# A graph-attention kernel on one core: inverse deviations by logarithm and exponential, hidden feed-forward rows in the score bank, and a new order on all engines

## What is computed

```python
q = (h @ Wq).reshape(n, 8, 64)
k = (h @ Wk).reshape(n, 8, 64)
v = (h @ Wv).reshape(n, 8, 64)
e = einsum('ehd,ehd->eh', k[src], q[dst]) / sqrt(64)
m = segment_max(e, dst)
ex = exp(e - m[dst])
attn = ex / segment_sum(ex, dst)[dst]
a = segment_sum(attn[:, :, None] * v[src], dst).reshape(n, 512)
x1 = layernorm(h + a @ Wo, ln1_g, ln1_b)
f = relu(x1 @ W1 + b1) @ W2 + b2          # inner width 64
layer = layernorm(x1 + f, ln2_g, ln2_b)
out = layernorm(x + layer)                # no gain, no bias
```

## Time and profile before

| | |
|---|---|
| median of three runs | 683.18 us (682.54 to 683.65) |
| profiled execution, its span | 682.0 us |
| PE busy | 641.5 us, 94% of the span |
| DVE busy | 578.0 us, 85% |
| ACT busy | 528.3 us, 77% |
| POOL busy | 401.7 us, 59% |
| mean granted clock of TensorE | 0.986 |
| moved by DMA | 91.44 MB, mean 134 GB/s |

### The profile page before, as it was taken

The page is one execution under the profiler, slowest core; times in us unless marked ns, Lnnn a source line. Parts: engine busy times, 40 slices in busy tenths (PEclk is TensorE's granted clock), DMA queues, the critical chain, the costliest instruction groups (busy, mean ns, idle before and its releaser), DMA issues. The chain is left out here.

```text
span 682.0 us, 10864 instructions
## 1 busy us (share of the span) xinstructions
PE 641.5 (94%) x3520; PEld 483.8 (71%) x3520; DVE 578.0 (85%) x1391; ACT 528.3 (77%) x1140; POOL 401.7 (59%) x363
## 2 busy tenths in 40 slices
PE   5999999999999999999999999999999999999950
PEld 2778877777777777777777777777778778675520
DVE  7668769879898898898889889988989898899792
ACT  2525269877888987988798889878878999698881
POOL 7267244867675865756776574864547726735423
PEclk9999999999999999999999999999999999999995
DMA  7844154644643745674474456455554824536452
GB/s 227 220 101 133 44 123 106 173 122 142 148 121 131 159 121 148 167 157 92 146 177 117 113 161 137 105 168 123 127 128 155 184 62 135 139 77 138 131 113 91
DMA packets 37747, 91.44 MB, mean 134 GB/s; under 512 B 8346, under 2 KB 9642, under 8 KB 37690
## 3 DMA queue, kind: packets, MB, share of 16 engines
q0 software_dynamic: 31536, 82.74, 47.6%
q1 hardware_dynamic: 6154, 8.01, 4.3%
HBM read 71.20 MB, written 20.99 MB: 135 GB/s over the span
## 5 line engine op out<-in xcount | busy, mean ns | idle before, releaser
L558 ACT ACTIVATE squares<-rows,nmean 125x512 bf16<-125x512 f32 x200 | 142.3, 713 | 41.5 <-DVE nmean L902 19.8
L412 POOL DMA_INDIRECT x_rows<-in_x_dram,node_idx x40 | 48.2, 1205 | 56.8 <-DVE rows L917 47.3
L416 POOL DMA_INDIRECT out_dram<-rows,node_idx x40 | 46.4, 1160 | 56.4 <-ACT rows L618 47.0
L473 POOL DMA_DIRECT2D x_rows<-in_L_gnn_ln_b_dram x40 | 52.9, 1372 | 31.1 <-DVE rows L821 21.7
L898 DVE SCALAR_TENSOR_TENSOR rows<-pF,rows 125x512 f32<-125x512 f32 x78 | 50.6, 686 | 23.2 <-PE pF L1103 22.5
L963 PE MATMUL pP<-wo_hi,aT_hi 128*125 128x512 f32 x160 | 65.9, 412 | 0.3 <-DVE aT_lo L848 0.3
L963 PE MATMUL pP<-xTs_hi,wv_hi 128*128 128x500 f32 x160 | 65.8, 411 | 0.0
L963 PE MATMUL pP<-xTd_hi,wq_hi 128*128 128x500 f32 x160 | 65.4, 409 | 0.1
L963 PE MATMUL pP<-xTs_hi,wk_hi 128*128 128x500 f32 x160 | 63.5, 397 | 0.6 <-ACT q L539 0.6
L963 PE MATMUL pP<-wo_lo,aT_hi 128*125 128x512 f32 x160 | 63.1, 394 | 0.0
L963 PE MATMUL pP<-wo_hi,aT_lo 128*125 128x512 f32 x160 | 63.0, 394 | 0.0
(11 more groups left out here) (197 smaller groups left out, 1760.6 us busy)
## 6 DMA issues: line engine op xcount, KB each, us to landing
x_rows<-in_L_gnn_ln_b_dram POOLq DMA_DIRECT2D x40, 512.0 KB, 6.7
dst_row<-in_dst_dram SPq DMA_DIRECT2D x9, 250.5 KB
q<-in_L_gnn_Wq_dram SPq DMA_DIRECT2D x1, 1024.0 KB, 5.6
rows<-in_L_gnn_Wk_dram SPq DMA_DIRECT2D x1, 1024.0 KB, 7.8
rows<-in_L_gnn_Wv_dram SPq DMA_DIRECT2D x1, 1024.0 KB, 6.8
x_rows<-in_L_gnn_Wo_dram SPq DMA_DIRECT2D x8, 128.0 KB, 6.0
xd<-in_x_dram,dst_idx POOLq DMA_INDIRECT x40, 4.6
xs<-in_x_dram,src_idx POOLq DMA_INDIRECT x40, 3.8
```

Of the source, the lines that this page charges most:

```text
L412: pool.indirect_dma_start(rows, None, x, bass.IndirectOffsetOnAxis(ap=table[:, column:column + 1].bitcast(U32), axis=0), bounds_check=N - ...
L416: pool.indirect_dma_start(out, bass.IndirectOffsetOnAxis(ap=table[:, column:column + 1].bitcast(U32), axis=0), rows, None, bounds_check=N ...
L473: pool.dma_start(xr_wide[n], bass.AP(tensor=be2.tensor, offset=be2.offset, ap=[[0, P], [0, 2], [1, D]]), accum_op=ALU.add).then_inc(s[f"be ...
L558: ins = act.activation(squares[:, t, :], w[n][:, t, :], ACT.Square, bias=nmean[c][n][:, t:t + 1], accum_out=sq[c][n][:, t:t + 1])
```

## The change

- **Inverse deviations.** ACT takes the logarithm of the variance plus epsilon (`Ln`), and in a step of its own the exponential of -0.5 times it. Both are in the table that softmax uses, and that table is loaded once, ahead of the rounds. The reciprocals on DVE and the 20 table loads of the rounds are gone.
- **Squares.** They take the row scaled by -512 with the row's sum as bias; the variance is scaled by 512 to the power of -3 in the logarithm. So the squares wait for the sum and not for the negative mean; two of the three scalings on DVE (`m1`, `m3`) are gone, and `nb1` and `shift` are made in one operation from the sum.
- **Hidden rows.** All 40 slots put them into `pS`, by turns into columns 0 to 124 and 125 to 249, the relu reads them into one of two buffers `hT`, and `F1` begins a new sum. No bank is cleared. The seeds of both `pF` banks are laid in one step of ACT. New waits on PE: `F1` waits until the round's weights have been read out of `pS` and until the job before has its relu; `S` waits for the relu of the last job ahead of it.
- **Order.** The tables have a time for each round and step, and `sequence` sorts by it. `FILLERS` have 256 columns and new places.

The core of the diff:

```diff
-TXD0 -189819 -22912 125030 125323 125345;
...
+TXD0 1441 4440 10800 13316 19562 25749 31284 37623 43613 49810;
...
+FILLERS = {(0, 'TURNF'): 16, (0, 'FOLD'): 12, (0, 'COUNT0'): 4, (0, 'COUNT1'): 4, (0, 'TXD1'): 8, (0, 'TXD3'): 6, (0, 'COUNT2'): 4, (8, 'E1.F1'): 18, (9, 'N1.T'): 36, (9, 'E1.T9'): 5}
...
+        for i, time in zip(rounds.get(step[0], range(ROUNDS)), times, strict=True):
+            due.append((int(time), i, step.strip("!<>")))
+    return [(i, step) for _, i, step in sorted(due)]
...
-        hT = sb("hT", [P, R])
+        hTs = [sb(f"hT{n}", [P, R]) for n in range(2)]
...
         def hidden(i, slot):
-            n = closing.index((i, slot))
+            n = job[i, slot] % 2
             return pS[:, R * n:R * n + R]
...
-            act.preload_act_table(ACT.Sqrt)
+            act.preload_act_table_set("natural_log_exp_and_others")
...
-                    act.preload_act_table_set(tables)
...
-                    act.preload_act_table(ACT.Sqrt)
...
-                        on.wait_ge(f"nm{c}", nth(f"dve.m{c}", slot, i))
...
-                            ins = act.activation(squares[:, t, :], w[n][:, t, :], ACT.Square,
-                                                 bias=nmean[c][n][:, t:t + 1], accum_out=sq[c][n][:, t:t + 1])
+                            ins = act.activation(squares[:, t, :], w[n][:, t, :], ACT.Square, scale=-float(D),
+                                                 bias=sums[c][n][:, t:t + 1], accum_out=sq[c][n][:, t:t + 1])
...
+                    def logarithm(c, var, scale):
+                        act.activation(lnv[c][n][:, :], var, ACT.Ln, bias=eps_col[0:R, :], scale=scale).then_inc(s[f"ln{c}"], 1)
...
+                    elif what == "sq":
+                        on.wait_ge("x2_done", 2 * nth("dve.x2", slot, i))
+                        squares_of(2)
...
+                            logarithm(c, sq[c][n][:, :], float(D) ** -3)
+                    elif what in ("rs1", "rs2", "rs3"):
+                        c = int(what[2])
+                        on.wait_ge(f"ln{c}", nth(f"act.ln{c}", slot, i))
+                        act.activation(rs[c][n][:, :], lnv[c][n][:, :], ACT.Exp, scale=-0.5).then_inc(s[f"rs{c}"], 1)
...
+                    elif what in ("F1", "F19"):
+                        before = job_before(i, slot, 2)
                         if before:
                             on.wait_ge("f_filled", 2 * nth("pe.F2", before[1], before[0]))
                         on.wait_ge("b1_done", 1)
                         on.wait_ge("h_filled", nth("pe.F1", slot, i))
+                        act.activation(hT_of(i, slot)[:, :], hidden(i, slot), ACT.Relu, bias=b1_col[:, :]).then_inc(s["h_done"], 1)
...
-                        act.activation(pF[0][:, 0:R], ident[:, 0:R], ACT.Copy, scale=0.0).then_inc(s["cleared"], 1)
...
+                        for t, bank in enumerate(f_banks(i, slot)):
+                            if before:
+                                on.wait_ge("x2_done", 2 * nth("dve.x2", before[1], before[0]) + t - 1)
+                            act.activation(bank[0:R, :], bias_all[0:R, :], ACT.Copy).then_inc(s["seeded"], 1)
...
-                        dve.reciprocal(rs[c][n][:, :], sd[c][n][:, :]).then_inc(s[f"rs{c}"], 1)
...
+                        dve.scalar_tensor_tensor(shift[n][:, :], sums[3][n][:, :], -1.0 / D, rs[3][n][:, :], ALU.mult, ALU.mult)\
+                            .then_inc(s["shifted"], 1)
...
                     on.wait_ge("weight_exp", i)
+                    if job_before_score[i]:
+                        j, slot = job_before_score[i]
+                        on.wait_ge("h_done", nth("act.F1", slot, j))
                     pe.matmul(pS[:, 0:EG], same_head[:, :], q[:, 0, 0:EG], start=True, stop=True).then_inc(s["score_done"], 1)
...
+                        on.wait_ge("weight_exp", scores_before[i, slot])
+                        before = job_before(i, slot)
+                        if before:
+                            on.wait_ge("h_done", nth("act.F1", before[1], before[0]))
                         for k in range(KC):
                             for t in range(2):
                                 ins = pe.matmul(hidden(i, slot)[DFF * t:DFF * t + DFF, :], w1[:, k, :], nT[:, k, R * t:R * t + R],
                                                 start=(k == 0), stop=(k == KC - 1))
```

More of the change, by code:

```diff
@@ L140, in sequence @@
     rounds = {"!": range(1), "<": range(ROUNDS - 1), ">": range(ROUNDS - 1, ROUNDS)}
-    for n, entry in enumerate(PLAN[engine].split(";")):
+    for entry in PLAN[engine].split(";"):
         step, *times = entry.split()
-        for i in rounds.get(step[0], range(ROUNDS)):
-            kind = i if i < 2 else max(2, i - ROUNDS + 5)
-            due.append((i * SLOT_PERIOD.get(step.strip("!<>").replace("GN", "N")[:2] if "." in step or "GN" in step else "", PERIOD) + int(times[kind] if len(times) > 1 else times[0]), i, n, step.strip("!<>")))
-    return [(i, step) for _, i, n, step in sorted(due)]
+        for i, time in zip(rounds.get(step[0], range(ROUNDS)), times, strict=True):
+            due.append((int(time), i, step.strip("!<>")))
+    return [(i, step) for _, i, step in sorted(due)]
 class Waits:
@@ L314, in pP_of, with job_before @@
             return pP[place[i, step] % 3]
-        def job_before(i, slot):
-            n = job[i, slot]
-            return jobs[n - 1] if n else None
+        def job_before(i, slot, back=1):
+            n = job[i, slot] - back
+            return jobs[n] if n >= 0 else None
+        scores_before = {}
+        job_before_score = {}
+        n_scores = n_jobs = 0
+        for i, step in pe_steps:
+            if step == "S":
+                job_before_score[i] = jobs[n_jobs - 1] if n_jobs else None
+                n_scores += 1
+            elif step.endswith((".F1", ".F19")):
+                scores_before[i, step.split(".")[0]] = n_scores
+                n_jobs += 1
         steps_done = {}
@@ L588, in _ @@
                                 .then_inc(s["nT_done"], 1)
-                    elif what == "F19":
-                        before = job_before(i, slot)
-                        on.wait_ge("f_filled", 2 * nth("pe.F2", before[1], before[0]))
-                        on.wait_ge("h_filled", nth("pe.F1", slot, i))
-                        act.activation(hT[:, :], hidden(i, slot), ACT.Relu, bias=b1_col[:, :]).then_inc(s["h_done"], 1)
-                    elif what == "F1":
-                        before = job_before(i, slot)
+                    elif what in ("F1", "F19"):
+                        before = job_before(i, slot, 2)
                         if before:
@@ L964, in split_product @@
                 return ins
-            for i, step in pe_steps:
+            for n_step, (i, step) in enumerate(pe_steps):
                 idle = FILLERS.get((i, step), 0)
```

475 lines of the change are left out of this document (301 added, 174 removed).

## The result

The changed kernel takes 693.39 us (median of four runs, 691.02 to 696.39) against 682.98; the ratio is 1.0152, with an interval of 1.0123 to 1.0180. It is 1.5% slower; 676.3, that is faster, had been forecast.

| us | before | after | difference | forecast |
|---|---|---|---|---|
| opening, to the first score matmul | 49.89 | 54.60 | +4.7 | +1.3 |
| nine rounds, to the tenth | 537.58 | 550.84 | +13.3 | -3.7 |
| end | 94.53 | 89.26 | -5.3 | -4.5 |

A forecast was written before the change was run, and what follows sets the result against it. PE was taken to set the pace in the nine rounds, DVE and ACT by turns the end. Opening +1.3, middle -3.7 and end -4.5 sum to -6.9; 683.18 - 6.9 = 676.3 us, range 673 to 680 (chance 0.50).

The forecast's parts named there:

- opening: Up to the first score matmul: +1.3 us, bounds -3.3 and +2.5, with PE idle some 3 us for source rows.
- end: From the tenth score matmul on: -4.5 us, DVE's 5.7 of removed work less ACT's 1.2 of added work.
- the middle: Nine rounds, first to tenth score matmul: -3.7 us, from PE's new order and fewer PE waits.
- The new order on PE: In the nine rounds: fewer costly changes between kinds of matmul on PE, 2.5 us less.
- 1.2 of PE's waits: In the nine rounds: with DVE relieved, 1.2 us of PE's waits go, taken between nothing and 2.5.
- the fourth rival: In the rounds: PE waits at the new hand-offs for ACT's relu, 1.4 us a round, 687.5 us; chance 0.10.
- The shift by 1.2: In the opening: gathers and Wv all move 1.2 us sooner (bounds 0 and 1.5), sources at 23.75.
- upper bound of +2.5: In the opening: its cost if nothing shifts sooner; a fall of the granted clock is not included.
- DVE's 3.7 + 2.0: In the end: DVE loses 22 reciprocals, 3.7 us, and twelve small scalings at 0.164, 2.0 us.
- DVE's waits: In the end: DVE waited 4.6 us for ACT's square roots; all of it comes off only in the -10.3 bound.
- Three of the four rivals: Opening, sources early: 671.7 us, chance 0.14; end fully DVE's: 670.5, 0.13; ACT sets the end: 682.0, 0.13.

The follow-up runs named there:

- pool3: The changed kernel with four steps of POOL's order moved ahead, among them round 7's gather of N0's rows ahead of the scatter of E0; 682.51 us.
- pool4: The changed kernel with pool3's POOL moves, but round 7's gather of N0's rows stays behind the scatter of E0, ahead of the mask; 680.50 us.
- pool4_open2: pool4 with the opening reordered: on PE four products go earlier, on ACT the first q tile is copied ahead of Wv's high part; 678.43 us.
- sqrt_back: pool4_open2 with the old arithmetic put back (roots on ACT, reciprocals on DVE, table loads around softmax); squares, hidden rows and order stay new; 703.68 us.
- gxs_only: The changed kernel with one exchange on POOL: round 6's source gathers and round 5's fill-index gathers change places; 691.55 us.
- old_end: pool4_open2 with the orders and fillers of before behind the tenth score matmul, computation new throughout; 686.32 us.
- new_end: old_order up to the tenth score matmul, and behind it the new orders and fillers; 682.38 us.
- old_order: The new computation in the orders of the kernel before on all engines, removed steps left out; 687.15 us.
- before_late: The kernel before with one step moved: on POOL the source gathers of round 6 stand behind the mask of round 5; 684.97 us.
- open_q: The changed kernel with PE's opening as it was, the first two products ahead of the first source transposes; 691.24 us.

## Why the prediction was wrong

- **The step that failed is the middle, and in it what was not in the sum: POOL.** The change rewrote the order on all engines, and the prediction priced PE's, ACT's and DVE's, not POOL's. "PE sets the pace" was read from a stretch in which every transfer had come early enough: in the kernel before the last source gather of round 6 is issued 26.8 us before PE is ready for it (344.26, 371.10); in the changed kernel 5.1. POOL's order could have been read before the result, as PE's was. Three late transfers and the clock behind them cost the 13.3 us; pool3 and pool4 take 10.7 and 13.5 back. In pool4, with the three gone, the kernel takes 680.5 and not 676.3: the rounds win 0.2 instead of 3.7, the opening loses 3.4 instead of 1.3, the end wins 5.3 instead of 4.5.
- **The new order on PE** was priced at -2.5, and 1.2 of PE's waits were to go. With POOL mended, the nine rounds take 537.3 to 537.8, as before (537.58). A round without any wait is indeed shorter: from the fourth score to the fifth 60.99, before 61.44. But the waits of PE of 0.25 us and more add up to 3.56 between first and tenth score in pool4_open2 and to 2.85 in pool4, before to 1.02: what the grouping saves, the shorter hand-offs take. That is the fourth rival (PE waits at hand-offs) at about a fifth of its price, 0.2 to 0.3 a round instead of 1.4. In the changed kernel no long wait is for the relu; the one for copied transposes (3.03) has the form that the rival names, but ACT was held there by a late gather and not by squares. In sqrt_back, with ACT heavier, PE does wait for the relu.
- **Opening.** The mechanism was right: PE idle 3.96 for the source rows, and a halved clock behind. The shift by 1.2 was not: the first destination gather is issued 1.4 sooner (6.27 instead of 7.68), but the last source gather only 0.4 (17.26 instead of 17.69), and the sources came at 26.1 where they had been there by 24.95. In pool3, pool4 and gxs_only, with the same opening, they came at 25.2, 24.8 and 25.0. Sum +4.7 in this profile instead of +1.3; by the three others +2.3 to +3.6, about the upper bound of +2.5, which left out the clock.
- **End.** -5.3 against -4.5: near in size, but by luck as far as the sum goes. DVE's 3.7 + 2.0 were durations (the four scalings of the first layernorm take 0.271 each and not 0.164, 0.4 more), and a small DVE instruction overlaps its neighbours: 24 reciprocals put back cost 1.3 of busy time and 0.8 of the end. And DVE's waits only moved: it waited 4.6 for roots, now 5.2 for ACT's exponentials:

```profile
L1089 DVE SCALAR_TENSOR_TENSOR shift<-sums,rs 125x2 f32<-125x2 f32 x8 | 1.2, 157 | 2.3 <-ACT rs L749 2.3
...
L1041 DVE SCALAR_TENSOR_TENSOR nb<-sums,rs 125x2 f32<-125x2 f32 x4 | 0.6, 161 | 2.9 <-ACT rs L749 2.9
```

  What shortened the end is two things together: the new tail (the order of the last 35 steps of PE, of those that feed them, and the fillers), worth 5.7 to 7.0 us with the new arithmetic (old_end, new_end), and the new arithmetic, worth 4.9 in the new order (sqrt_back) and nothing in the old one (old_order). The prediction summed the second as if it paid in any order. Which part of the arithmetic does it, the chain through DVE or ACT's loads, stays open.
- **The chances.** 0.10 was left for slower. Three of the four rivals took the middle's -3.7 as given, and the fourth looked for the waits at the hand-offs; none named a late transfer.

## What to carry to other kernels

Where a change rewrites the order of several in-order queues, go through every queue, that of the DMA issuer first: for each transfer read its margin, from issue to the moment at which its first user is ready, before the change, and how far behind waiting steps it stands now. Hold that margin against the longest landing in the trace and not the median (here 8.3 to 12.5 us against 3.8 and 7.0). A bottleneck engine at 17.00 of 17 says that it is fed, not that it will stay so. Price a stall of TensorE (PE) with the slow matmuls that can follow it, and a removed small instruction by what its neighbours then do, not by its duration. And where a change has two parts, ask whether one pays without the other.

## What was not expected of the hardware

- A stall of PE in mid-kernel costs up to about twice its length: 3.27, 2.07 and 3.03 us were each followed by slow matmuls (behind the first a second feed-forward group took 2.00, 376.62 to 378.62, instead of 1.06), and so was 1.93 in old_order; 1.44 in before_late and 1.42 in pool3 were not. The length alone does not decide it: 1.87 in sqrt_back (at 420.48) was followed by them too, 1.87 and 1.98 in open_q and 2.81 in pool3's opening (at 25.24) were not.
- The eight loads of Wo take SP (SyncE) 4.77 us to issue in the changed kernel and 3.72 before. It goes with the arithmetic, not with the order: 4.74 to 4.90 in all kernels with logarithm and exponential, 3.71 in before_late and 3.91 in sqrt_back with roots. The diff leaves SP's part as it was; why it is so stays open. In old_order, where Wo came late, the opening was 3.0 us longer than before; in new_end, with the same opening and 4.86, PE waited 0.60 instead of 1.93 and the opening was 1.9 longer, so not all of the 3.0 is Wo's.

```profile
27.42 4.77 SPq L538 DMA_DIRECT2D x_rows<-in_L_gnn_Wo_dram  x8
```
```profile
26.45 3.71 SPq L373 DMA_DIRECT2D x_rows<-in_L_gnn_Wo_dram  x8
```
```profile
25.07 3.91 SPq L543 DMA_DIRECT2D x_rows<-in_L_gnn_Wo_dram  x8
```
